# Paged attention on one core: value pages requested as two half-page transfers, each gated on its own half of the buffer

## The reference

```python
B, S, HID = (64, 32, 512)            # as it is called here
D, HQ, HK = (128, 32, 8)
PAGES, PSIZE, NPP = (64, 32, 16)
...
L = NPP * PSIZE                      # 512 cached keys
kc = k_cache[block_table].reshape(bsz, L, HK, D)
vc = v_cache[block_table].reshape(bsz, L, HK, D)
k_all = jnp.concatenate([kc, k], axis=1)
v_all = jnp.concatenate([vc, v], axis=1)
valid_c = jnp.arange(L)[None, :] < cache_seqlens[:, None]
...
scores = jnp.einsum('bqhd,bkhd->bhqk', q, k_all) * SCALE
scores = jnp.where(valid[:, None, None, :], scores, -1e+30)
probs = jax.nn.softmax(scores, axis=-1)
o = jnp.einsum('bhqk,bkhd->bqhd', probs, v_all)
```

## Time and profile before

| | |
|---|---|
| median of 3 runs | 2616.27 us (2610.56 to 2620.38) |
| the profiled execution | 2625.55 us, its span 2624.0 us |
| TensorE busy, whole span | 2441.7 us (93%) |
| VectorE, ScalarE, GpSimd busy | 1807.7, 1592.3, 428.6 us |
| mean granted TensorE clock | 0.971 |
| moved by DMA | 541.09 MB, mean 206 GB/s |
| attention: first key page issued | 952.07 us |
| attention: last matmul starts | 2220.65 us |
| transfers of key pages / value pages | 1024 / 1024, of 128 KB each |

### The profile page before, as it was taken

One profiled execution on the slowest core, in us unless ns is written; L12 is line 12 of the kernel. 1 busy time (PEld: TensorE's weight loads), 2 busy tenths in 40 slices (PEclk: granted clock), 3 DMA queues, 4 the chain that ended last, 5 costly groups with the idle time before them and its releaser, 6 DMA issues. The chain is left out here.

```text
span 2624.0 us, 57577 instructions
## 1 busy us (share of the span) xinstructions
PE 2441.7 (93%) x16326; PEld 2210.3 (84%) x16327; DVE 1807.7 (69%) x3636; ACT 1592.3 (61%) x3277; POOL 428.6 (16%) x625
## 2 busy tenths in 40 slices
PE   6699799999999949999999999999999998599999
PEld 5578588877878839999999999999999998388887
DVE  5345336999999948887887778878777785544443
ACT  3122235777777848888888878878788785311111
POOL 1222231010001011222222222222222221000000
PEclk9899899999999979999999999999999999799999
DMA  6422342333333369999999999899999995756664
GB/s 220 148 74 75 124 140 84 97 103 99 100 94 92 89 192 257 294 283 285 290 281 291 282 286 279 276 290 281 279 289 279 275 292 148 275 204 216 219 216 152
DMA packets 388288, 541.09 MB, mean 206 GB/s; under 512 B 61667, under 2 KB 275363, under 8 KB 384356
## 3 DMA queue, kind: packets, MB, share of 16 engines
q1 hardware_dynamic: 352932, 450.10, 56.2%
q0 software_dynamic: 33152, 87.07, 10.2%
q10 hardware_dynamic: 2112, 2.89, 0.4%
HBM read 441.54 MB, written 98.30 MB: 206 GB/s over the span
## 5 line engine op out<-in xcount | busy, mean ns | idle before, releaser
L1514 PE MATMUL att_ps_o<-att_pt,att_v 128*128 128x128 f32 x4096 | 544.2, 276 | 23.0 <-DMA att_v<-in_v_pages 20.8
L1514 PEld LDWEIGHTS att_ps_o<-att_pt,att_v 128*128 128x128 f32 x4096 | 506.0, 192 | 28.5 <-issue 22.2
L1333 ACT ACTIVATE att_prob<-att_prob,att_shift 128x544 f32<-128x544 f32 x512 | 383.7, 749 | 210.0 <-DVE att_shift L1399 196.8
L76 PE MATMUL att_ps_s<-att_k_hi,att_q_hi 128*128 128x272 f32 x1024 | 339.3, 331 | 34.2 <-DVE att_k_lo L1430 22.4
L1399 DVE CUSTOM_DVE_ANT_0 att_prob<-att_ps_s,att_mask 128x544 f32<-128x544 f32 x512 | 366.5, 716 | 0.0
L1430 DVE TENSOR_TENSOR att_k_lo<-att_k_raw,att_k_hi 128x1024 fp32r<-128x1024 f32 (+1 forms) x320 | 338.5, 1058 | 19.6 <-ACT att_k_hi L1348 19.6
L76 PE MATMUL qkv_ps_y<-qkv_w_hi,qkv_xt_hi 128*128 128x512 f32 x768 | 316.2, 412 | 0.0
L1340 ACT ACTIVATE att_pt<-att_ps_pt 128x512 f32<-128x512 f32 x512 | 295.5, 577 | 31.9 <-PE att_ps_pt L1493 30.4
L1493 PE MATMUL att_ps_pt<-att_ident,att_prob 128*128 128x128 f32 x2048 | 309.5, 274 | 1.1 <-ACT att_pt L1340 1.1
L1348 ACT ACTIVATE att_k_hi<-att_k_raw 128x1024 fp32r<-128x1024 f32 (+1 forms) x320 | 292.8, 915 | 28.0 <-DMA att_k_raw<-in_k_pages 28.0
L78 PE MATMUL qkv_ps_y<-qkv_w_hi,qkv_xt_lo 128*128 128x512 f32 x768 | 302.6, 394 | 0.0
(11 more groups left out here) (178 smaller groups left out, 4688.1 us busy)
## 6 DMA issues: line engine op xcount, KB each, us to landing
att_k_raw<-in_k_pages SPq DMA_DIRECT2D x1024, 128.0 KB, 2.9
att_v<-in_v_pages SPq DMA_DIRECT2D x1024, 128.0 KB, 4.3
q_t<-qkv_out_t SPq DMA_DIRECT2D x128, 256.0 KB, 2.3
att_q_raw<-q_t POOLq DMA_DIRECT2D x64, 512.0 KB, 6.6
o_t<-att_o POOLq DMA_DIRECT2D x64, 512.0 KB, 7.4
out_o<-o_t SPq DMA_DIRECT2D x32, 1024.0 KB, 6.2
out_inv<-inv_t SPq DMA_DIRECT2D x32, 1024.0 KB, 6.5
qkv_w_stage<-in_w_qkv SPq DMA_DIRECT2D x12, 1024.0 KB, 5.2
```

What stands on the lines that cost most here:

```text
L76: pe.matmul(out, xh, wh, start=start, stop=False)
L1333: act.activation(prob[:, b, :], prob[:, b, :], ACT.Exp, bias=shift[:, b:b + 1], scale=-1.0, accum_out=total[:, j // HK, j % HK:j % HK + 1] ...
L1514: pe.matmul(out, v_sb[:, p, c, h * DH:(h + 1) * DH], pt_sb[:, j % OG, c, :], start=(c == 0), stop=False)
```

## The change

Three edits:

1. `load_v` gets a fourth argument `half`. It loads heads 0 to 3 or 4 to 7 of all 16 value pages (32 keys x 512 floats, 64 KB), each half behind its own wait: heads 0 to 3 of the sequence two earlier multiplied for half 0, all 8 for half 1. So 32 transfers of 64 KB take the place of 16 of 128 KB.
2. The order in SP's loop: for each sequence s, V(s+1) half 0, then K(s+2), then V(s+1) half 1. `pages_in` is called ahead of each of the three, so three times a sequence instead of three times a pair.
3. `v_loaded` becomes four semaphores (buffer x half), and PE waits ahead of head 0 for half 0 and ahead of head 4 for half 1. To have semaphores for that, the table, lengths and key numbers share one (`small_loaded`), and lengths and masks share one (`lens_and_masks`).

```diff
-        v_loaded = m.sems("v_loaded", 2)
+        v_loaded = [m.sems(f"v_loaded{p}_", HK // OG) for p in range(2)]
...
-                def load_v(s, p, pages):
-
+                def load_v(s, p, pages, half):
+
+
+                    heads = slice(half * OG * DH, (half + 1) * OG * DH)
                     if later(s, 2):
-                        sp.wait_ge(pv_done, HK * (s - 1))
+                        sp.wait_ge(pv_done, HK * (s - 2) + OG * (half + 1))
                     for n in V_ORDER:
                         at = n % PPP * PSIZE
-                        sp.dma_start(v_sb[at:at + PSIZE, p, n // PPP, :], v_pages[bass.ds(pages[n], 1)])\
-                          .then_inc(v_loaded[p], 16)
-
-                sp.dma_start(table_sb[:, :], table).then_inc(table_loaded, 16)
-                sp.wait_ge(table_loaded, 16)
+                        sp.dma_start(v_sb[at:at + PSIZE, p, n // PPP, heads], v_pages[bass.ds(pages[n], 1), :, heads])\
+                          .then_inc(v_loaded[p][half], 16)
+
+                sp.dma_start(table_sb[:, :], table).then_inc(small_loaded, 16)
+                sp.wait_ge(small_loaded, 48)
                 pages = pages_in(0)
                 load_k(0, 0, pages)
-                load_v(0, 0, pages)
+                for half in range(HK // OG):
+                    load_v(0, 0, pages, half)
                 load_k(1, 1, pages_in(1))
 
                 def pair(i, last):
 
-                    if not last:
-                        next_pages = pages_in(2 * i + 2)
-                        load_k(2 * i + 2, 0, next_pages)
-                    load_v(2 * i + 1, 1, pages_in(2 * i + 1))
-                    if not last:
-                        load_k(2 * i + 3, 1, pages_in(2 * i + 3))
-                        load_v(2 * i + 2, 0, next_pages)
+
+                    for p in range(2):
+                        s = 2 * i + p
+                        if not (last and p):
+                            load_v(s + 1, 1 - p, pages_in(s + 1), 0)
+                        if not last:
+                            load_k(s + 2, p, pages_in(s + 2))
+                        if not (last and p):
+                            load_v(s + 1, 1 - p, pages_in(s + 1), 1)
...
-                    if h == 0:
-                        pe.wait_ge(v_loaded[p], 16 * NPP * (i + 1))
+                    if h % OG == 0:
+                        pe.wait_ge(v_loaded[p][h // OG], 16 * NPP * (i + 1))
+                    if h == 0:
                         pe.wait_ge(own_v_loaded[p], 16 * OG * (i + 1))
```

More of the change, by code:

```diff
@@ L1187, in attention @@
         ps_o = m.ps("ps_o", [P, 2, OG, P])
-        zeroed, ident_ready, table_loaded = m.sem("zeroed"), m.sem("ident_ready"), m.sem("table_loaded")
-        small_loaded, lens_ready, mask_ready = m.sem("small_loaded"), m.sem("lens_ready"), m.sem("mask_ready")
+        zeroed, ident_ready = m.sem("zeroed"), m.sem("ident_ready")
+        small_loaded, lens_and_masks = m.sem("small_loaded"), m.sem("lens_and_masks")
         q_loaded, own_k_loaded, own_v_loaded, o_stored, inv_stored = pool_sems
@@ L1371, in _ @@
             def _(dve):
-                dve.wait_ge(small_loaded, 32)
-                dve.tensor_copy(lens_f[:, :], lens_sb[:, :]).then_inc(lens_ready, 1)
-                dve.wait_ge(lens_ready, 1)
+                dve.wait_ge(small_loaded, 48)
+                dve.tensor_copy(lens_f[:, :], lens_sb[:, :]).then_inc(lens_and_masks, 1)
+                dve.wait_ge(lens_and_masks, 1)
                 dve.wait_ge(zeroed, 2)
@@ L1379, in make_mask @@
                     dve.tensor_scalar(mask[:, p, 0:NKEY], key_sb[:, :], lens_f[:, bass.ds(s, 1)], MASKED,
-                                      ALU.is_ge, ALU.mult).then_inc(mask_ready, 1)
-                    dve.wait_ge(mask_ready, s + 1)
+                                      ALU.is_ge, ALU.mult).then_inc(lens_and_masks, 1)
+                    dve.wait_ge(lens_and_masks, s + 2)
                 def wait_for_scores(s, u, j):
```

## The result

The changed kernel takes **3207.7 us** (median of 4 runs, 3205.2 to 3209.4) where the kernel before takes 2616.5 us: ratio 1.226, 95% interval 1.224 to 1.229, so 591 us slower. The forecast was 3174 us, slower, with a range of 3090 to 3250 us.

A forecast was written before the change was run, and what follows sets the result against it. SP's issuing was taken to bound the kernel, not the wait for a free buffer. Steady part 535 us, start 26 and end -3 sum to 558 us; added to the 2616.3 us median, 3174 us, range 3090 to 3250 us.

The forecast's parts named there:

- SP's issuing is the pace of the kernel before: In attention, SP's queue issues without pause at 19.46 us a sequence, more than PE's 18.7 us, so it sets the pace.
- A half-page issue costs 0.50 us, whatever its size: On SP, each half-page value transfer holds the queue 0.50 us like a whole one: 16.0 us a sequence for both halves.
- Table reads at 1.2 us: On SP, three table reads a sequence instead of one and a half, 1.2 us each: 3.6 us a sequence.
- The keys are late next: In attention, ScalarE waits for keys about 9.7 us a sequence, 580 us; PE's waits on values go to about zero.
- The clock does not decide: Against a rival (5%, up to 3690 us) where PE's idle time lowers its clock and PE becomes the bound.
- start: In attention's first sequences, added value issues and table reads bring the keys of sequence 3 26 us later.
- steady part: Over 60 sequences of attention, SP needs 28.4 us each for 19.5 before: 535 us more.
- end: From the last keys' start to the last matmul, 50 to 53 us instead of 54: 3 us less.
- I take them as gone: Long value instructions on SP, 1.2 us a sequence, vanish as DMA share falls to about 0.64; if all stayed, 3244 us.
- the jams: Value instructions on SP of up to 1795 ns, where the DMA engines are behind: 1.2 us of the 19.46 a sequence.
- 18.3 without them: SP's time a sequence in the kernel before without its long value instructions: 8.65 + 7.7 + 1.8 + 0.15 us.
- theory B: From the experiments: SP's own work is 18.3 us, the other 1.2 us waits on full DMA engines that added work swallows.

The follow-up runs named there:

- t2: The kernel before with 2 more transfers of 4 bytes a sequence on SP, ahead of the values: 2682.8 us, ratio 1.026.
- t6: The kernel before with 6 more transfers of 4 bytes a sequence on SP, ahead of the values: 2764.6 us, ratio 1.057.
- p2: The kernel before with 2 of each sequence's 16 value pages issued from POOL's queue instead of SP's: 2596.9 us, ratio 0.992.
- p4: The kernel before with 4 of each sequence's 16 value pages issued from POOL's queue instead of SP's: 2594.5 us, ratio 0.9925.
- e2: The kernel before with each value page as two 64 KB transfers and one more table read a pair of sequences, order and waits kept: 3140.7 us, ratio 1.200.
- e3: The changed kernel with the keys of s+2 issued ahead of both value halves of s+1: 3204.5 us.
- v_half_bytes: The kernel before with value pages loaded for heads 0 to 3 only, same number of transfers, half the value bytes: 2611.2 us, ratio 0.997.
- the control: The kernel before with one first-layer wait of PE bounded, an edit all the study's kernels carry: 2619.5 us, ratio 1.0015.

## Why the prediction was right

By its own steps:

- *SP's issuing is the pace of the kernel before*: shown from both sides. More issues lengthen it (t2, t6), two or four fewer make PE the bound (p2, p4).
- *A half-page issue costs 0.50 us, whatever its size*: 316 ns of instruction, 16 in 7.8 us at the start (986.10 to 993.93 us). Perfetto Trace Analysis of the Trainium skill (DMA Optimizations) names generally idle DMA engines as the case in which splitting may help. Before the change their share was 0.94, so this was not that case, and no run here splits with idle engines at hand. With the split the share is lower, 0.68 in e2 and 0.64 in the changed kernel, and the time over 500 us longer: the engines have less to do because SP feeds them more slowly. The 50 ns of dispatch in DMA: Bandwidth & Descriptors of the Trainium skill (Anatomy of one DMA), a figure for GpSimd's path, is not what an issue holds SP for (316 ns), nor POOL, whose page issues take 499 ns in p4; the trace does not tell the parts of an issue from each other.
- *Table reads at 1.2 us*: e3 against e2 gives 1.24 us.
- *The keys are late next*: 598 us at L1353, 570 more than before, for the 580 forecast; PE's waits for values went to 0.
- *The clock does not decide*: PE stands some 8 us in each sequence and the granted clock is 0.86 over the long stretch. Between 1510 and 1520 us PE is busy for 5.75 of 10 us, and then it is almost wholly at its lower level, 1.2 GHz:

```profile
1520.00:1530.00 10.00, 5.69 (x30) 5.69 (x31) 5.83 (x12) 7.15 (x14) 0.00 (x0) 0.55 0.72 205
```

The 8491 matmuls would take 974 us at the rate of 1050 to 1100 us and took 1101 us busy: 127 us over 52 sequences, 2.4 us each, for which there was idle time. The row agrees with TensorE: Matmul & The Clock Gate of the Trainium skill (Part 1: The HAM clock gate), by which idle time brings the half rate back.

- *The sum*, in the profiled executions: start 25.8 us (forecast 26), steady part 60 x 9.41 = 564 us (535), end 7 us less (3 less; last matmul 47.5 us after the last keys' start, 54.0 before). Together 583 us for 558. The start is right partly by luck: the keys of sequence 1 come 5.9 us later (forecast 8), and from there to sequence 3 it is 19.8 us more (18.4). A further 8 us of the 34 between forecast and median are no step of the kernel: the forecast took the profiled execution to lie 9.3 us above the median, as before, and the new one lies 1.3 us above.

**The term that was mis-sized** is the steady one, 28.86 for 28.4 us, and in it the step "I take them as gone", said of the jams. Summed as in t2, the time of page issues and table reads beyond their usual length was 1.6 us a sequence before and is 0.5 us now. That is the whole difference: without it the pace is 28.3 us. The reason given for the jams, "where the DMA engines are behind", did not hold: with the share down to 0.75 (v_half_bytes) they are as large as in the control, 1.5 us, and with it up at 1.02 (p2) they are 0.6 us. What follows from "18.3 without them", that SP has work of 18.3 us and the rest is waiting that added work would take the place of, was spelled out as theory B, and t2 refuted it. What does make single issues take 0.5 to 2.5 us stays open; no run here separates the number of transfers in flight from their packets or from POOL's bursts.

## What to carry to other kernels

Before splitting a transfer to start it sooner, add up the time of the queue that issues it: here 32 issues of about 0.5 us, the table reads and the long instructions filled the whole period of 19.5 us, although no line of the page called SP busy. An issue costs nearly the same for 4 bytes (0.42 to 0.50 us) and for 64 KB (0.50 us), so halving the size of transfers nearly doubles the bill, and the gain has to be larger than that. If such a queue is the pace, move a few of its issues to an idle queue: two to four pages in sixteen were worth 21 us, where neither the order nor the earlier wait gave anything.

## What was not expected of the hardware

- The issue time on SP hardly depends on size: in the median 233 to 300 ns for 4 bytes, 316 to 332 ns for 64 KB, 331 to 370 ns for 128 KB.
- Issuing instructions stretch, to 2.5 us at most, and the total does not follow the DMA share: 1.5 us a sequence at 0.75 as at 0.95, 0.6 us at 1.02.
- Two queues together held a DMA share of 1.00 at 293 GB/s over 1050 us in p4 without making anything late. SP alone reached 0.94 over that stretch, though 1.01 at 291 GB/s between 1050 and 1100 us.
